# One transformer layer with routed experts on one core: the first late group's turned rows kept in DRAM, and its shared product moved beside the last expert tile

## The reference

```python
x = x + layernorm(attn(layernorm(x)))      # attn: QKV, rotation, sum over tokens of cos(K)*V, times Q, W_out
xf = layernorm(x).reshape(-1, 512)
logits = xf @ gate_w                       # 8 experts
gates = softmax of the two largest logits
h = gelu(einsum('nd,edh->neh', xf, w1) + b1)          # h has 256 columns
routed = einsum('ne,ned->nd', gates, einsum('neh,ehd->ned', h, w2) + b2)
shared = gelu(xf @ shared_w1 + shared_b1) @ shared_w2 + shared_b2   # 512 -> 512 -> 512
x = x + layernorm(routed + shared)
```

## Time and profile before

| | |
|---|---|
| median of 3 runs | 947.52 us (944.09 to 948.36) |
| profiled execution | 946.99 us |
| its span | 945.2 us |
| instructions | 14783 |
| busy: PE, DVE, ACT, POOL | 93%, 68%, 46%, 42% of the span |
| mean granted TensorE clock | 0.979 |
| expert tiles | 71, from about 594 to 858 us |
| the end (late groups) | about 858 to 945 us |
| last tile's turn on PE (1831) | 855.4 us |
| issue of the load of `c2_raw` | 859.8 us |
| issue of the last output store | 941.3 us |

### The profile page before, as it was taken

One profiled execution on the slowest core, in us unless ns is written; L12 is line 12 of the kernel. 1 busy time (PEld: TensorE's weight loads), 2 busy tenths in 40 slices (PEclk: granted clock), 3 DMA queues, 4 the chain that ended last, 5 costly groups with the idle time before them and its releaser, 6 DMA issues.

```text
span 945.2 us, 14783 instructions
## 1 busy us (share of the span) xinstructions
PE 881.7 (93%) x4558; PEld 727.5 (77%) x4558; DVE 639.3 (68%) x1370; ACT 436.1 (46%) x829; POOL 396.6 (42%) x321
## 2 busy tenths in 40 slices
PE   4999999999999989999999886899999899998985
PEld 3788787788888677777777775788888789886864
DVE  6967977977956756576576585366656566664877
ACT  5335445345243132231313553466666566664564
POOL 1456557557454000000000000468767577762175
PEclk9999999999999999999999988799999999999998
DMA  8328878878658984658522988498879889787999
GB/s 302 113 89 295 316 258 302 304 267 307 238 206 323 364 288 189 245 176 309 177 99 87 385 335 211 108 228 152 144 143 164 195 147 167 145 128 181 361 188 214
DMA packets 87626, 209.03 MB, mean 221 GB/s; under 512 B 11496, under 2 KB 19944, under 8 KB 82432
## 3 DMA queue, kind: packets, MB, share of 16 engines
q1 hardware_dynamic: 62592, 162.29, 47.8%
q0 software_dynamic: 19360, 43.60, 25.8%
q10 hardware_dynamic: 5600, 2.20, 1.2%
HBM read 117.05 MB, written 91.01 MB: 220 GB/s over the span
## 4 chain that ended last, share of the span: by engine, by line
PE 47%; issue 10%; DVE 8%; ACT 4%; DMA 2%; POOL 1%; POOLq 0%; DVEq 0%; ACTq 0%; SPq 0%
PE bank L1824 4%; PE bank L1822 3%; PE bank L1823 3%; PE bank L1580 3%; PE bank L1809 3%; PE bank L1581 3%; PE bank L1582 3%; PE bank L1839 3%; PE bank L1841 3%; PE bank L1840 3%; PE bank L1831 2%; PE bank L1575 2%; DMA f_scratch<-ro,dst 2%; PE bank L1730 2%; PE bank L1731 2%
## 5 line engine op out<-in xcount | busy, mean ns | idle before, releaser
L1529 POOL DMA_INDIRECT f_scratch<-ro,dst x71 | 112.5, 1584 | 57.2 <-issue 19.0
L1521 POOL DMA_INDIRECT xr<-n_scratch,ids x71 | 70.0, 986 | 79.8 <-issue 56.8
L1580 PE MATMUL bank<-wkv_hi,h_hi 128*128 128x512 f32 x248 | 97.2, 392 | 0.2 <-DVE vb L951 0.2
L1582 PE MATMUL bank<-wkv_hi,h_lo 128*128 128x512 f32 x248 | 96.6, 389 | 0.0
L1581 PE MATMUL bank<-wkv_lo,h_hi 128*128 128x512 f32 x248 | 96.5, 389 | 0.0
L1319 DVE TENSOR_TENSOR ro<-bank,b2b 128x512 f32<-128x512 f32 x71 | 49.1, 692 | 69.0 <-PE bank L1841 54.1
L1822 PE MATMUL bank<-we,x_hi 128*128 x284 | 87.0, 306 | 0.2 <-DVE x_lo L1299 0.2
L1824 PE MATMUL bank<-we,x_lo 128*128 x284 | 81.2, 286 | 0.0
L1823 PE MATMUL bank<-we,x_hi 128*128 x284 | 81.1, 286 | 0.0
L633 ACT ACTIVATE sq<-kb 128x512 f32<-128x512 f32 x32 | 20.2, 633 | 127.8 <-DVE kb L946 127.8
L1839 PE MATMUL bank<-we,g_hi 128*128 x142 | 56.7, 399 | 4.2 <-DVE g_lo L1311 4.2
(11 more groups left out here) (242 smaller groups left out, 2526.3 us busy)
## 6 DMA issues: line engine op xcount, KB each, us to landing
xg<-in_X SPq DMA_DIRECT2D x15, 1024.0 KB, 7.5
we<-expert_scratch SPq DMA_DIRECT2D x6, 2048.0 KB, 13.1
w_lo<-in_w SPq DMA_DIRECT2D x16, 512.0 KB, 5.6
expert_scratch<-w_hi SPq DMA_DIRECT2D x16, 512.0 KB, 2.8
expert_scratch<-w_lo SPq DMA_DIRECT2D x16, 512.0 KB, 4.3
q_scratch<-qh SPq DMA_DIRECT2D x8, 1024.0 KB, 3.9
q_scratch<-qb SPq DMA_DIRECT2D x8, 1024.0 KB, 6.4
q_hi<-q_scratch SPq DMA_DIRECT2D x8, 1024.0 KB, 5.1
```

Of the source, the lines that this page charges most:

```text
L1521: pool.indirect_dma_start(xr[u][:, :], None, n3_dram, bass.IndirectOffsetOnAxis(ids[:, i:i + 1], 0)).then_inc(row_in[u], 16)
L1529: pool.indirect_dma_start(f_dram, bass.IndirectOffsetOnAxis(dst[:, i:i + 1], 0), ro[i % NRO][:, :], None, compute_op=ALU.add).then_inc(r_s ...
L1580: pe.matmul(dst, hi(k), w_hi(k), start=(k == 0), stop=False)
L1582: last = pe.matmul(dst, lo(k), w_hi(k), start=False, stop=(k == KD - 1 and not more))
```

## The change

- The second stage's `n_hi` and `n_lo` of late group 0 (group 1) are stored by SP in step 2 to a new DRAM scratch, two stores of 1 MB. The semaphore is `turned`, and ACT waits for it before it writes `n_hi` in step 3.
- In the experts SP loads the high part (`nc_hi[0]`) where it loaded `n3c0`. The low part and `c1_lo` come in halves of 512 KB: low part after the landing of tile 32's scatter, `c1_lo` after 34, low part after 36, `c1_lo` after 38. `n3c1` is now loaded after tile 64's scatter has landed (before: after 32).
- The turns, copies and subtractions of late group 0 are gone: 16 transposes on PE, 4 copies on ACT, 4 subtractions on DVE.
- PE does the first eight matmuls of h(0) between the last tile's turn and its second product, where it waits for `g_hi` and `g_lo`; the rest follows the last tile. `n3c1` is turned after column block 1 (before: after all eight-matmul parts), and each block's low part comes right behind its high part.
- Buffers and PSUM banks are given out anew, and SP loads the rows of late group 1 of `f_scratch` only after group 1's turns.

```diff
+    nt_dram = dram("turned_scratch", (2, P, KD * G))
...
-        tc = (bank[1], bank[0], bank[7], bank[2])
-        sc = bank[3:7]
+        tc = ((bank[7], bank[2], bank[5], bank[6]), (bank[1], bank[0], bank[7], bank[2]))
+        sc = (bank[0], bank[1], bank[3], bank[4])
...
+                if s == LATE[0] + 1:
+                    sp.wait_ge(t2_free, 2 + t2_use(LATE[0], KD - 1) + 1)
+                    for c, part in enumerate((n_hi, n_lo)):
+                        sp.dma_start(nt_dram[c], part[:, :, :].rearrange("p k t -> p (k t)").bitcast(F32)).then_inc(turned, 16)
...
-            load_n3(0)
+            sp.wait_ge(turned, 32)
+            sp.dma_start(nc_hi[0][:, :, :].rearrange("p k t -> p (k t)").bitcast(F32), nt_dram[0]).then_inc(turned, 16)
...
                 if i == NT:
                     sp.wait_ge(oe_full, NT)
+                if i in (NT, NT + 4):
+                    c = (i - NT) // 4 * 2
+                    sp.dma_start(nc_lo[0][:, c:c + 2, :].rearrange("p k t -> p (k t)").bitcast(F32), nt_dram[1, :, c * G:(c + 2) * G])\
+                      .then_inc(c_in[0], 16)
+                if i in (NT + 2, NT + 6):
+                    c = (i - NT) // 4 * 2
+                    sp.dma_start(c1_lo[:, c:c + 2, :].rearrange("p k h -> p (k h)").bitcast(F32), ws_dram[0, 1, :, c * SH:(c + 2) * SH])\
+                      .then_inc(c_in[0], 16)
+                if i == NRT - E:
+                    sp.wait_ge(oe_full, NRT - E)
                     load_n3(1)
-                    sp.dma_start(c1_lo[:, :, :].rearrange("p k h -> p (k h)").bitcast(F32), ws_dram[0, 1]).then_inc(c_in[0], 16)
...
+                    if g == LATE[0] + 1 and k == 0:
+                        act.wait_ge(turned, 32)
                     act.activation(n_hi[:, k, :], tp[n % 2][:, :], ACT.Copy).then_inc(n_hi_done, 1)
...
-                else:
-                    pe.wait_ge(n3c_in[0], 32)
-                    pe.wait_ge(xt_free, PRE)
-                    late_turn_part(0, 0)
                 h_of(i, u, e)
-                if i == PRE:
-                    late_turn_part(0, 1)
                 o_of(i - 1, 1 - u, e_before)
-            pe.wait_ge(th_free, 2 + PRE)
-            late_turn_part(0, 2)
             h_turn(PRE, PRE % 2)
-            o_of(PRE, PRE % 2, e)
-            late_turn_part(0, 3)
...
+            pe.wait_ge(xt_free, PRE + 1)
+            pe.wait_ge(turned, 64)
+            pe.wait_ge(c_in[0], 64)
+            late_h_part(0, 0, False)
+            o_of(PRE, PRE % 2, e)
             def late_h(i):
-                pe.wait_ge(tc_free, 4 + KD * (i + 1))
                 if i == 0:
-                    for m in range(KS):
-                        if m == 2:
-                            pe.wait_ge(oe_free, 2 + NRT - 1)
+                    late_h_part(0, 0, True)
+                    late_h_part(0, 1, False)
+                    late_h_part(0, 1, True)
+                    pe.wait_ge(hc_free, NRT - 1)
+                    pe.wait_ge(th_free, 2 + NRT - 1)
+                    pe.wait_ge(oe_free, 2 + NRT - 1)
+                    late_turn(1)
+                    for m in range(2, KS):
                         late_h_part(i, m, False)
-                    late_turn(1)
-                    pe.wait_ge(c_in[0], 16)
-                    for m in range(KS):
                         late_h_part(i, m, True)
                     return
```

More of the change, by code:

```diff
@@ L215, in sandwich_kernel @@
         f = [at(f"f{g}", kb_, [P, GT, D]) for g, kb_ in enumerate((64, 104, 16, 24, 32, 40, 48, 56))]
-        n3c = [at(f"n3c{i}", kb_, [P, GT, D]) for i, kb_ in enumerate((128, 0, 72))]
-        nc_hi, nc_lo = ([at(f"{n}{i}", kb_, [P, KD, G], F32R) for i, kb_ in enumerate(kbs)] for n, kbs in (("nc_hi", (80, 164)), ("nc_lo", (88, 96))))
+        n3c = [None, at("n3c1", 8 * LATE[1], [P, GT, D]), at("n3c2", 72, [P, GT, D])]
+        nc_hi, nc_lo = ([at(f"{n}{i}", kb_, [P, KD, G], F32R) for i, kb_ in enumerate(kbs)] for n, kbs in (("nc_hi", (128, 164, 80)), ("nc_lo", (0, 96, 88))))
         c1_hi, c1_lo = at("c1_hi", 136, [P, KD, SH], F32R), at("c1_lo", 8, [P, KD, SH], F32R)
@@ L586, in _ @@
                     sp.wait_ge(oe_full, NT)
+                if i in (NT, NT + 4):
[8 more added lines that the diff above has]
+                    sp.wait_ge(oe_full, NRT - E)
                     load_n3(1)
-                    sp.dma_start(c1_lo[:, :, :].rearrange("p k h -> p (k h)").bitcast(F32), ws_dram[0, 1]).then_inc(c_in[0], 16)
             def load_x2(g):
                 sp.dma_start(x2c[g][:, :, :], out_groups[g]).then_inc(n3c_in[ADDED.index(g)] if g in ADDED else f_in[g], 16)
-            for g in EARLY[:2] + LATE[:1] + EARLY[2:] + LATE[1:2]:
+            for g in EARLY[:2] + LATE[:1] + EARLY[2:]:
                 load_f(g)
+            sp.wait_ge(tc_full, KD)
+            load_f(LATE[1])
             sp.wait_ge(c_split, KS)
             load_f(LATE[2])
-            sp.wait_ge(tc_full, KD * len(LATE))
+            sp.wait_ge(tc_full, KD * (len(LATE) - 1))
             for g in ADDED:
@@ L820, in nc_hi_part @@
             def nc_hi_part(i, k):
-                act.wait_ge(tc_full, KD * i + k + 1)
-                if i == 2 and k == 0:
-                    act.wait_ge(sc_full, KS)
-                act.activation(nc_hi[i % 2][:, k, :], tc[k][:, :], ACT.Copy).then_inc(nc_hi_done, 1)
+                act.wait_ge(tc_full, KD * (i - 1) + k + 1)
+                act.activation(nc_hi[i][:, k, :], tc[i - 1][k][:, :], ACT.Copy).then_inc(nc_hi_done, 1)
             act.wait_ge(o_full, NO)
@@ L851, in gelu_c @@
                     act.wait_ge(hc_split, n - 1)
-                act.activation(hsc[m % 2][:, :], sc[m if i == 0 else m % 2][:, :], ACT.Gelu, bias=sb1c[:, m:m + 1]).then_inc(sc_free, 1)
+                act.activation(hsc[m % 2][:, :], sc[m if i == 0 else 2 + m % 2][:, :], ACT.Gelu, bias=sb1c[:, m:m + 1]).then_inc(sc_free, 1)
                 if m == 0 and i > 1:
@@ L1321, in nc_lo_part @@
             def nc_lo_part(i, k):
-                dve.wait_ge(nc_hi_done, KD * i + k + 1)
-                dve.tensor_tensor(nc_lo[i % 2][:, k, :], tc[k][:, :], nc_hi[i % 2][:, k, :].bitcast(F32), ALU.subtract)\
+                dve.wait_ge(nc_hi_done, KD * (i - 1) + k + 1)
+                dve.tensor_tensor(nc_lo[i][:, k, :], tc[i - 1][k][:, :], nc_hi[i][:, k, :].bitcast(F32), ALU.subtract)\
                    .then_inc(tc_free, 1)
@@ L1341, in _ @@
                     x_lo_part(i + 1, 1 - u)
-                else:
-                    nc_lo_part(0, 0)
                 h_out(i, u, e)
                 o_out(i - 1, 1 - u, e_before)
-            nc_lo_part(0, 1)
             g_lo_part(PRE, PRE % 2)
-            nc_lo_part(0, 2)
             o_out(PRE, PRE % 2, e)
-            nc_lo_part(0, 3)
             def nc_lo_parts(i):
@@ L1395, in add_x2 @@
                 if j == 0 and g in ADDED:
-                    dve.wait_ge(n3c_in[ADDED.index(g)], 48 if g == ADDED[0] else 32)
+                    dve.wait_ge(n3c_in[ADDED.index(g)], 80 if g == ADDED[0] else 32)
                 dve.wait_ge(y_normed, y_use[g, j] + 1)
@@ L1847, in late_turn_part @@
             def late_turn_part(i, k):
-                pe.wait_ge(tc_free, KD * i + k + 1)
-                transposes(tc[k], n3c[i], k).then_inc(tc_full, 1)
+                pe.wait_ge(tc_free, KD * (i - 1) + k + 1)
+                transposes(tc[i - 1][k], n3c[i], k).then_inc(tc_full, 1)
             pe.wait_ge(owner_ready, 1)
@@ L1883, in late_h_part @@
             def late_h_part(i, m, lo):
-                c, u = slice(m * P, (m + 1) * P), i % 2
-                dst = sc[m if i == 0 else m % 2][:, :]
+                c = slice(m * P, (m + 1) * P)
+                dst = sc[m if i == 0 else 2 + m % 2][:, :]
                 if lo:
                     for k in range(KD):
-                        last = pe.matmul(dst, c1_lo[:, k, c], nc_hi[u][:, k, :], start=False, stop=(k == KD - 1))
+                        last = pe.matmul(dst, c1_lo[:, k, c], nc_hi[i][:, k, :], start=False, stop=(k == KD - 1))
                     last.then_inc(sc_full, 1)
```

14 lines of the change are left out of this document (5 added, 9 removed).

## The result

The changed kernel took 936.45 us (median of 5 runs, 935.16 to 938.13), the kernel before on the same occasion 944.15 us (5 runs, 941.94 to 948.36): ratio 0.9916, 95% interval 0.989 to 0.9941. Run again later, 12 times beside 28 runs of before, it took 935.57 against 940.82: ratio 0.9947, interval 0.9926 to 0.9968. So it is faster, by 5 to 8 us in the medians, and both intervals lie under 1.

What follows compares the result with a forecast made beforehand. TensorE, busy 93% of the span, was taken as the bound, with full DMA engines limiting the tail. From the profiled 946.99, less 2.6 (experts) and 1.9 (end), came 942.5, or 943.0 us as median; range 939.7 to 947.8.

Steps and rivals of the forecast that it cites:

- The experts' loads: Change of expert: spacing the loads as halves removes most of TensorE's 2.84 us wait, gaining 2.6 us.
- The harm of the halves: Experts: first half lengthens a scatter by about half of 0.8 us overlap; each later half costs a scatter 1.3 us.
- The weight at the second late group: End: c2_raw takes 9.8 us, so the second group starts at 872.2, 3.1 us earlier.
- a rival: End: c2_raw lands early, at 865.4; TensorE gains 6.6 us, the time 5, giving 939.9; chance 0.15.
- the end's gain: After the last tile: 2.1 us by compute, 1.2 to 2.1 by the last store; 1.9 us taken.
- The tail: Outputs: DMA engines full from 899, f loads 0.5 us later, DMA work ends about 1.2 us earlier.
- only the dip, 1.7 us: Between f loads and first outputs: the free DMA time a full tail can save, 1.7 us.
- The clock: TensorE, after about 3.5 us idle before the second late group: lower clock costs 1.0 us.
- The second stage: Step 2: two new 1 MB stores delay VectorE's fo copy some 2 us; cost to the time 0.
- the cover of 2.5 us: Second stage: slack between ScalarE's norms and TensorE's need, 2.5 us; delay beyond it costs one for one.
- The base: Whole kernel: forecast starts from the profiled 946.99 us and the median of 947.52 us.

Runs made afterwards that it cites:

- e1: Kernel before with only the experts' two 1 MB loads split into four halves, after tiles 32, 34, 36 and 38: 937.77 us, ratio 0.9965.
- e3: Changed kernel with the c2_raw load issued behind all four copies of late group 1 on ScalarE: 941.70 us, ratio 1.0011.
- e10: Kernel before with the c2_raw and n3c2 loads issued one tile earlier, behind tile 69's ro copy: 941.66 us, ratio 1.0007.
- after again: Changed kernel, unchanged, run again beside more runs of the kernel before: 935.57 us, ratio 0.9947.
- e2: Changed kernel with nc_lo's and c1_lo's halves made whole 1 MB loads again, both after tile 32's scatter: 938.18 us, ratio 0.9964.
- e8: Changed kernel with VectorE's last two statistics and their variance moved behind an addition TensorE stood for: 935.55 us, ratio 0.9942.
- e4: Changed kernel with the c2_raw and n3c2 loads issued earlier, behind the last tile's gelu: 934.11 us, ratio 0.9936; again 933.25 us, ratio 0.9923.
- e6: Changed kernel with the eight matmuls of h(0) behind the last tile's second product, not in front: 936.15 us, ratio 0.995.
- e9: Changed kernel with e4's and e8's edits, and the turned-row stores behind step 2's first two fo stores: 931.68 us, ratio 0.9903; again 930.04 us, 0.9879.
- e11: Changed kernel with the c2_raw and n3c2 loads issued behind the first of late group 1's four copies: 940.22 us, ratio 0.9985.

## Why the prediction was wrong

*The experts' loads (2.6 us).* Right: 2.6 us between the means of the traces with the pair and with the halves (239.9 less 237.3), 3.4 in the profiled pair. The mechanism was as said: POOL's wait of 7.6 us is 3.35. The harm of the halves was laid in the wrong place. The first one, which the text had at 3.3 us beside 0.8 us of a scatter, took 5.6 to 7.4 us where its landing can be read, and scatter 34 took 5.4 us in two traces and 6.7 to 7.6 in nine; the second one, for which the text had 1.3 us, cost scatter 35 at most 0.4 us. In e1 and e3 TensorE still waited 1.5 to 1.65 us at that place.

*The weight at the second late group.* This is the step that failed. The text took 9.8 us for `c_raw` because the row of before said so, and so 872.2 for the second group's start, 3.5 us of idle time and 1.0 us of clock. The load took 6.2 us (5.7 to 6.2 in five profiles of the new end), the group followed with no idle time, and the clock stayed at 1.00. From the turn it started 7.1 us earlier (27.8 to 20.7), not 3.1. The 9.8 us were no property of the load: they were those of a load behind the packets of two scatters. From the turn the change moved the load 1.3 us earlier and scatter 69 1.1 us later (11.5 to 12.6), and so its packets came first. The text had seen that the load "now meets the last scatters later" and gave this outcome 0.15 as a rival, with 6.6 us for TensorE, 5.0 for the time and 939.9 in all; the end's gain was 5.2 in the profiled pair and 4.6 between means (97.1 of before, e1, e10; 92.5 of after, after again, e2). The Trainium skill's formula (DMA: Bandwidth & Descriptors, Anatomy of one DMA), which gives an estimate of about 4.4 us and which the page measured for DMAs issued from GpSimd, was nearer than the row, and lower than all measured here from ScalarE: 5.5 us at best.

*The tail.* The text let a full tail save "only the dip, 1.7 us", from a DMA share of 1.08. It gave up 4.6 to 5.2 of the 7.1 us. A full share was no bound on the work done: at 1.02 276 GB/s went through, where before, at 1.00, it was 258. By the rule of the experiments the tail of before could have ended 91 to 92.4 us from the turn (22.5 and 68.5 to 69.9, an estimate), and it ended at 97.65 because TensorE was late. There was a bound, but as e8, e4 and e6 show it is the time from the first `f` load, and that moved later by 1.2 us from the turn (22.5 to 23.7 or 23.9), where the text had 0.5: the last scatters pay for the weight.

*The clock.* No fall where the text had one. One came elsewhere: of eleven profiles with the same idle time of 1.8 us before a second product of the tail (named at the end) four showed it. It cost 1.7 us of TensorE and, in this tail, nothing of the span: after again had no fall and the same end (92.60 against 92.44).

*The second stage (0).* The stores held `fo` for 3.35 us, not 2, and the cover of 2.5 us was passed by 0.9: TensorE stood 0.90 us. It cost nothing in the end, since TensorE stands for 9 us in front of the first tile with these stores or without them (8.6 to 9.4 in all profiles): the first turn of x came at 592.7 us (mean of the nine profiles with these stores in front, 591.1 to 594.1) and at 592.6 in the three old ones. The Trainium skill's rule on a ring's order (DMA: Bandwidth & Descriptors, Queues, rings and completion order), by which its descriptors are taken in their order and which the text named for this wait, agrees with the 9.5 us of that store and with the wait's going in e9.

*The base.* The other half of the miss. The forecast was a gain of 4.5 us from 947.52, the median of 3 runs; over 5, 26, 28 and 23 runs before's median was 944.15, 941.52, 940.82 and 942.25. Of the 6.6 us between 943.0 and 936.45, 3.4 are this base (947.52 less 944.15) and 3.2 the gain (7.7 less 4.5). As a ratio the forecast was 0.995, near the 0.9947 of the larger comparison, but this nearness is in part luck: its end was worth 1.9 us where the traces have 4.6, so that the spans of the parts come to 7.2 us, not 4.5. The larger comparison (3.0 to 7.0 us by its interval) can't say how much of the difference arrives in the time. The profile had a warning in it, a clock at half until 604 us in a stretch that no argument used.

## What to carry to other kernels

The time that a load took in a profile belongs to its place: look at which queue's packets share the engines with it, and ask whether the change moves it ahead of them and who pays. Here a shift of 2.4 us against the scatters took 3.6 us off a load. A DMA share of 1 says that the engines are occupied, not that the stretch can't shrink; compare GB/s, and look for the transfer from which the rest counts. Before forecasting a time to 0.5%, ask how far the runs of the base spread (here 936.6 to 948.4 us): the gain can be known better than the time.

## What the runs showed of the hardware

The clock after a like idle time is not the same in each execution. In after again TensorE stood 1.85 us and the clock stayed:

```profile
902.82 0.50 PE L1592 MATMUL bank<-c_hi,hc_hi 128*128 128x512 f32 x1 [1.85 <-DVE f L1401]
```

```profile
903.00:911.00 8.00, 8.00 (x36) 6.60 (x37) 7.04 (x24) 4.61 (x7) 7.55 (x12) 1.00 1.13 215
```

In after, with 1.84 us, it fell:

```profile
907.00:915.00 8.00, 7.13 (x24) 5.73 (x25) 5.89 (x20) 2.65 (x4) 6.31 (x9) 0.79 1.12 236
```

It fell to the same 0.79 in e2, e3 and e4 and stayed at 1.00 in before, e1, e10, e6, e11 and the second profile of e4. The last three scatters behind two loads of 1 MB took 8.5 to 9.4 us each (after, after again), and 4.9 to 6.1 with the loads 5 us further ahead (both profiles of e4): the same bytes, another order.
